# Two-layer cross-attention on one core: a new written-out order for the four engines, and one wait fewer

## The reference

```python
# layer 0 (x1 = x[b], x2 = ctx[b]); D = 64
q = x1^T Wq^T + bq ;  k = Wk x2 + bk ;  v = Wv x2 + bv
x = v @ softmax(q k)^T + x1
# layer 1 (CI = 256, no softmax, so it is linear)
g = g_w x2 + g_b ; theta = theta_w x + theta_b ; phi = phi_w x2 + phi_b
y = ((theta^T phi) / N) g^T ;  out = batchnorm(w_w y^T + w_b) + x
```

## Time and profile before

| | |
|---|---|
| median of 3 runs | 1082.88 us (1082.83 to 1083.77) |
| the profiled execution | 1082.83 us, span 1081.0 us |
| TensorE matmul busy | 1051.3 us, 97% of the span |
| VectorE, ScalarE, GpSimd busy | 688.5, 466.0 and 279.1 us |
| granted TensorE clock, mean | 0.997 of full speed |

### The profile page before, as it was taken

How to read it: one execution, slowest core, us unless ns; L and a number is a source line. 1 busy time by engine, 2 the same in 40 slices (tenths; PEclk the granted TensorE clock), 3 DMA queues, 4 the chain that set the end, 5 groups by cost and what they waited for, 6 DMA issues and landing times.

```text
span 1081.0 us, 14139 instructions
## 1 busy us (share of the span) xinstructions
PE 1051.3 (97%) x5272; PEld 871.0 (81%) x5272; DVE 688.5 (64%) x929; ACT 466.0 (43%) x794; POOL 279.1 (26%) x198
## 2 busy tenths in 40 slices
PE   5899999999999999999999999999999999999997
PEld 4688877888788887888878888788887888778886
DVE  6785387843878438773487735876368762787615
ACT  7543254433554345443544335443255432555411
POOL 0311243112521125112360114502254022440120
PEclk9999999999999999999999999999999999999999
DMA  8224352352513525136142442424424343243402
GB/s 284 98 72 132 118 175 67 73 152 99 191 44 76 163 93 176 46 82 204 60 156 59 110 163 69 147 71 110 151 78 137 78 115 139 84 136 74 137 20 78
DMA packets 80627, 122.07 MB, mean 113 GB/s; under 512 B 13104, under 2 KB 46384, under 8 KB 80560
## 3 DMA queue, kind: packets, MB, share of 16 engines
q1 hardware_dynamic: 80560, 121.17, 36.2%
HBM read 70.79 MB, written 16.78 MB: 81 GB/s over the span
## 4 chain that ended last, share of the span: by engine, by line
PE 83%; DVE 8%; DMA 5%; issue 2%; ACT 1%; SPq 0%; POOL 0%; DVEq 0%; ACTq 0%; POOLq 0%
PE pG L549 32%; PE pG L469 12%; PE pG L460 11%; PE pG L560 8%; DMA out_dram<-xr 4%; PE pG L489 4%; PE pS L501 3%; DVE xr L862 2%; PE pM L528 2%; PE pT L501 2%; PE pM L537 2%; DVE xr L857 2%; PE pT L450 1%; PE pT L570 1%; PE pG L570 1%
## 5 line engine op out<-in xcount | busy, mean ns | idle before, releaser
L549 PE MATMUL pG<-pt,vT 128*128 128x512 f32 x1536 | 352.6, 390 | 0.5 <-DVE pt L812 0.5
L549 PEld LDWEIGHTS pG<-pt,vT 128*128 128x128 f32 x1536 | 287.4, 188 | 59.7 <-issue 0.9
L460 PE MATMUL pG<-wv,x2s 128*128 128x512 f32 x768 | 183.1, 394 | 3.2 <-DVE vT L765 2.7
L460 PEld LDWEIGHTS pG<-wv,x2s 128*128 128x128 f32 x768 | 143.5, 189 | 36.7 <-DVE vT L765 5.7
L841 DVE SCALAR_TENSOR_TENSOR xr<-pG,cl,xr 128x512 f32<-128x512 f32 x64 | 48.0, 750 | 190.0 <-PE pG L549 185.9
L891 POOL TENSOR_TENSOR xms<-xr,xms 128x512 fp32r<-128x512 f32 x64 | 86.1, 1346 | 315.9 <-ACT xms L698 315.9
L469 PE MATMUL pG<-x2Ts 128*128 128x256 f32 (+2 forms) x768 | 129.3, 326 | 0.0
L469 PEld LDWEIGHTS pG<-x2Ts 128*128 128x128 f32 x768 | 115.7, 189 | 10.3 <-issue 2.9
L698 ACT ACTIVATE xms<-xr 128x512 fp32r<-128x512 f32 x64 | 40.3, 630 | 185.9 <-DVE xr L841 185.8
L883 POOL TENSOR_TENSOR x2Ts<-x2T_f,x2Ts 128x512 fp32r<-128x512 f32 x64 | 91.2, 1456 | 90.6 <-ACT x2Ts L645 90.5
L887 POOL TENSOR_TENSOR ys<-yf,ys 128x256 fp32r<-128x256 f32 x32 | 26.6, 830 | 310.2 <-ACT ys L666 309.7
(11 more groups left out here) (104 smaller groups left out, 1276.8 us busy)
## 6 DMA issues: line engine op xcount, KB each, us to landing
mv<-tp SPq DMA_DIRECT2D x512, 64.0 KB, 2.0
st<-in_ctx_dram SPq DMA_DIRECT2D x32, 512.0 KB, 5.8
st<-in_x_dram SPq DMA_DIRECT2D x32, 512.0 KB, 3.5
x2T_f<-in_ctx2T_dram SPq DMA_DIRECT2D x32, 512.0 KB, 6.0
xr<-in_x_dram SPq DMA_DIRECT2D x64, 256.0 KB, 3.2
out_dram<-xr SPq DMA_DIRECT2D x64, 256.0 KB, 2.7
wv_f<-in_wvT_dram SPq DMA_DIRECT2D x4, 256.0 KB, 6.5
wpg_f<-in_wpgT_dram SPq DMA_DIRECT2D x1, 1024.0 KB, 6.0
```

Of the source, the lines that this page charges most:

```text
L460: last = mm(bank, x2s[:, l, c, 128 * m:128 * m + 128], wv[:, r, c, :], start=(c == 0 and n == 0), stop=(c == 3 and n == 2))
L549: last = mm(bank, vT[:, l, m, 128 * c:128 * c + 128], pt(h)[:, r, m, :], start=(m == 0 and n == 0), stop=(m == 7 and n == 2))
```

## The change

All four order strings of `FIRST` and of `LATER` are replaced, and ScalarE's `do_q` loses a wait. No step is added or removed; only positions change, and for `x1:1` to `x1:3`, `x2:3` and `xs:3` the batch in whose string they stand. The parts near the end of a batch (`LATER`):

```diff
 pe (start of the batch)
-"q:0 k:0 q:1 k:1 v:0 gs v:1 v:2 S:0 S:1 gt G:0 S:2 S:3 G:1 G:2 GT:0 G:3 v:3 v:4 GT:1 S:4 S:5 v:5 ..."
+"k:0 q:0 q:1 k:1 v:0 v:1 v:2 gs S:0 S:1 G:0 S:2 S:3 G:1 G:2 gt G:3 v:3 S:4 S:5 GT:0 GT:1 v:4 v:5 ..."
 act (start)
-"x1:1 x1:2 x2:3 x1:3 xs:3 s q x2T:0 k x2T:1 x2T:2 x2T:3 v:0 x2T:4 x2T:5 x2T:6 q2 v:1 k2 gs x2T:7 v:2 gt ..."
+"q s x2T:0 x2T:1 k v:0 k2 q2 x2T:2 x2T:3 x2T:4 x2T:5 v:1 v:2 x2T:6 x2T:7 gs S:0 S:1 G:0 S:2 G:1 gt ..."
 act (end)
-"... PV:0,0 PV:0,1 T:4 T:5 T:6 T:7 B:0 B:1 PV:0,2 PV:0,3 PV:1,0 PV:1,1 PV:1,2 +x2:0 PV:1,3 +x2:1
- th:0,0 +xs:0 +x2:2 th:0,1 +xs:1 +x1:0 th:1,0 +xs:2 th:1,1"
+"... T:4 T:5 T:6 T:7 PV:0,0 PV:0,1 PV:0,2 PV:0,3 PV:1,0 PV:1,1 B:0 B:1 +x2:0 +x2:1 th:0,0 PV:1,2 +x2:2
+ PV:1,3 th:0,1 +xs:0 +xs:1 +x2:3 +xs:2 th:1,0 th:1,1 +x1:0 +x1:1 +x1:2 +x1:3 +xs:3"
 dve (start)
-"q k v:0 q2 k2 v:1 S:0 S:1 n:0 tr:0 v:2 n:1 tr:1 G:0 S:2 S:3 ..."
+"s q k v:0 k2 q2 v:1 v:2 S:0 S:1 n:0 tr:0 S:2 G:0 n:1 tr:1 G:1 S:3 ..."
 dve (end)
-"... B:0 B:1 PV:0,3 PV:1,0 PV:1,1 PV:1,2 PV:1,3 +x2:0 +x2:1 th:0,0 +x2:2 th:0,1 th:1,0 th:1,1
- wy:0,0 out:0,0 wy:0,1 out:0,1 wy:0,2 wy:0,3 wy:1,0 +x2:3 wy:1,1 out:0,2 out:0,3 out:1,0 out:1,1
- +s wy:1,2 wy:1,3 out:1,2 out:1,3"
+"... PV:0,3 PV:1,0 PV:1,1 PV:1,2 PV:1,3 B:0 B:1 +x2:0 th:0,0 +x2:1 +x2:2 th:0,1 th:1,0 th:1,1 +x2:3
+ wy:0,0 out:0,0 wy:0,1 out:0,1 wy:0,2 wy:0,3 out:0,2 out:0,3 wy:1,0 wy:1,1 out:1,0 out:1,1
+ wy:1,2 wy:1,3 out:1,2 out:1,3"
 pool
-"x1:0 x1:1 x1:2 x1:3 x2T:0 ... PV:1,3"
+"x2T:0 ... PV:1,3 +x1:0 +x1:1 +x1:2 +x1:3"
```

`FIRST` changes in the same manner. At its start:

```diff
 pe
-"k:0 k:1 v:0 v:1 q:0 q:1 gs v:2 v:3 S:0 v:4 S:1 S:2 gt G:0 G:1 GT:0 S:3 S:4 G:2 ..."
+"k:0 k:1 v:0 v:1 q:0 q:1 v:2 v:3 gs S:0 S:1 gt v:4 S:2 G:0 S:3 G:1 G:2 G:3 GT:0 ..."
 dve
-"x2:0 x2:1 x2:2 w:0 x2:3 consts w:1 w:2 x1:0 w:3 w:4 x1:1 x1:2 w:5 x1:3 s v:0 k w:6 w:7 w:8 q v:1 k2 q2 v:2 ..."
+"x2:0 x2:1 x2:2 w:0 x2:3 consts w:1 x1:0 w:2 w:3 w:4 w:5 x1:1 x1:2 s k x1:3 v:0 v:1 w:6 w:7 w:8 q k2 q2 v:2 ..."
```

and at its end, on ScalarE and VectorE:

```diff
 act
-"... PV:1,2 +x2:0 PV:1,3 +x2:1 th:0,0 +xs:0 +x2:2 th:0,1 +xs:1 +x1:0 th:1,0 +xs:2 th:1,1"
+"... PV:1,0 +x2:0 +x2:1 PV:1,1 PV:1,2 th:0,0 B:1 PV:1,3 th:0,1 +xs:0 +x2:2 +x2:3 th:1,0 +xs:1 th:1,1
+ +x1:0 +x1:1 +xs:2 +xs:3 +x1:2 +x1:3"
 dve
-"... th:1,1 wy:0,0 out:0,0 wy:0,1 out:0,1 wy:0,2 wy:0,3 wy:1,0 +x2:3 wy:1,1 out:0,2 out:0,3 ..."
+"... +x2:0 +x2:1 th:0,0 B:1 th:0,1 +x2:2 +x2:3 th:1,0 th:1,1 wy:0,0 wy:0,1 out:0,0 wy:0,2 out:0,1
+ out:0,2 wy:0,3 out:0,3 wy:1,0 wy:1,1 ..."
```

The wait:

```diff
             def do_q(b):
                 wait(eng, "q", b, 1)
-                if b:
-                    wait(eng, "oa", b - 1, 3)
                 done(act(q1[0:64, :], pT[64:128, :, :], ACT.Copy), "t1q")
```

More of the change, by code:

```diff
@@ L80 @@
         "x2T:0 x2T:1 x2T:2 x2T:3 x2T:4 x2T:5 x2T:6 x2T:7 Y:0 Y:1 Y:2 Y:3 PV:0,0 PV:0,1 PV:0,2 PV:0,3 PV:1,0 "
-        "PV:1,1 PV:1,2 PV:1,3"
+        "PV:1,1 PV:1,2 PV:1,3 +x1:0 +x1:1 +x1:2 +x1:3"
     ),
@@ L86 @@
     pe=(
[4 rows of a table removed]
[4 rows of a table added]
     ),
     act=(
[4 rows of a table removed]
[4 rows of a table added]
     ),
     dve=(
[5 rows of a table removed]
[5 rows of a table added]
     ),
     pool=(
-        "x1:0 x1:1 x1:2 x1:3 x2T:0 x2T:1 x2T:2 x2T:3 x2T:4 x2T:5 x2T:6 x2T:7 Y:0 Y:1 Y:2 Y:3 PV:0,0 PV:0,1 PV:0,2 "
-        "PV:0,3 PV:1,0 PV:1,1 PV:1,2 PV:1,3"
+        "x2T:0 x2T:1 x2T:2 x2T:3 x2T:4 x2T:5 x2T:6 x2T:7 Y:0 Y:1 Y:2 Y:3 PV:0,0 PV:0,1 PV:0,2 PV:0,3 PV:1,0 "
+        "PV:1,1 PV:1,2 PV:1,3 +x1:0 +x1:1 +x1:2 +x1:3"
     ),
```

## The result

The changed kernel takes 1101.45 us (median of 4 runs, 1100.64 to 1102.7), the kernel before 1082.86 us on the same chip: a ratio of 1.0171, with a 95% interval from 1.0153 to 1.0188. It is slower by 18.6 us. The forecast was 1098 us, in a range of 1079 to 1106, with 0.76 for slower.

What follows compares the result with a forecast made beforehand. TensorE's matmuls, busy 97% of the span, were taken as the bound. Terms +18.0 (six boundaries), -0.6 (out of batch 0), -1.0 (start) and -1.4 (end) gave +15.0 on 1082.8: 1098 us, range 1079 to 1106.

Steps and rivals of the forecast that it cites:

- forecast case: VectorE and GpSimd block each other at batch boundaries, TensorE stalls; 1098 us, own range 1092 to 1103, chance 0.48.
- step 1: End of a batch: GpSimd's late PV tiles delay th:0,1's low part, so th:1,1 stalls 1.9 to 2.0 us.
- faster: Rival: VectorE and GpSimd don't meet at the boundary, only the cures are left; 1072 us, chance 0.18.
- middle: Rival: no stall before th:1,1, only the wy stalls, +1.4 us for each of six boundaries; 1088 us, chance 0.22.
- Six boundaries: Boundaries out of LATER: +3.0 us taken for each, +18.0 in all.
- the start: First batch: the 2.69 us stall goes, S:0 waits some 3 us instead; -1.0, between -2 and +2.
- the end: Last batch: two fewer out between the last matmul and the last two evictions; -1.4, between -1.5 and 0.
- the boundary out of batch 0: th:1,1 isn't held up, wy stalls are smaller, the 1.6 before S:0 goes; net -0.6, between -1.5 and +2.
- the worked-out +3.4: One boundary's sum: k:1 over 4.0 us later, less the 0.6 wait before S:0 that goes.
- a bound for `T:3`: DMAs some 3 us later make T:3 ready 0.2 us before to 0.4 after PV:0,0 wants it.
- Step 4: qhi, qlo, khi, klo ready about 6.6 us after k:1, before v and gs end, so the 0.6 before S:0 goes.
- The removed wait: The wait taken from do_q on ScalarE is always met by the new order: 0 us.

Runs made afterwards that it cites:

- pv_split_early: The changed kernel, but ScalarE splits PV:1,2 and PV:1,3 before and between x2:0 and x2:1 again in batches 1 to 7: 1092.61 us.
- x1_zero: The changed kernel, but GpSimd writes zeros into x1's low part by memset in batches 1 to 7 and reads nothing: 1079.2 us.
- starts_new: The changed kernel with ScalarE's and VectorE's batch ends (from PV:1,0 on) as in the kernel before, wait in do_q kept: 1110.2 us.
- out_behind_wy: The changed kernel, but out:0,2 and out:0,3 behind wy:1,0 and wy:1,1 on VectorE in batches 1 to 7, wait in do_q back: 1108.6 us.
- before_cured: The kernel before with, in batches 1 to 7, k:0 before q:0, and k2 before q2, both ahead of x2T tiles on ScalarE: 1081.49 us.
- cured_sp: before_cured with the next batch's loads x2T:2 and x2T:3 issued behind the stores of out:1,0 to out:1,3 in SP's queue: 1072.8 us.
- end_new: The kernel before with only the ends of the batches changed (ScalarE and VectorE from PV:1,0 on): 1120.33 us.

## Why the prediction was right

**The forecast case happened, at the places named.** TensorE waits before `th:1,1`, `wy:1,2` and `q:0`; four `out` of over 2 us stand at a boundary and not two; no wait of L501 on `klo`. The block between VectorE and GpSimd is shown by the run without GpSimd's reads, step 1 by `pv_split_early`. The "faster" and the "middle" case each needed one of these to be absent.

**The terms.** Six boundaries were set at +18.0 and came to +21.8; the start at -1.0 and came to -1.24; the end at -1.4 and came to -1.53; the boundary out of batch 0 at -0.6, and it came to +0.88. The total was set at +15.0 and came to +19.9 in the profiled executions. The mean period out of `LATER` is 135.4, where 134.8 was written.

Split at `S:0`, the terms tell something else (change against the kernel before, us; from `PV:0,0` to the first `th` nothing changes):

| | forecast | came to |
|---|---|---|
| first `th` to `S:0`, six boundaries | +18.0 (+20.4 as worked out) | +15.5 |
| first `th` to `S:0`, out of batch 0 | -0.6 | -0.83 |
| `S:0` to `PV:0,0`, batches 2 to 7 | 0 | +6.3 |
| `S:0` to `PV:0,0`, batch 1 | 0 | +1.68 |

So the boundaries cost less than was worked out, the middles of the batches cost 8.0 us that the sum didn't have, and the two errors partly cancel. That the total came within 4 us of 1101.45 is in part luck: with the middles in it, the same sum would have been 1106, the upper end of the range. The boundary out of batch 0 itself came out as forecast, although `wy:1,3` waits 1.53 us there (at 150.35) for `wy:0,3`, which stands behind three `out`, two of them blocked; what makes it +0.88 is the middle of batch 1.

**Within a boundary** the worked-out +3.4 up to `S:0` was too much: it is 2.57 in the one followed. Step 1 was put at 1.9 to 2.0 and is 1.28 against the kernel before. Most of that error can be read: GpSimd starts 0.17 us sooner than worked out, and the blocked instructions follow each other every 1.1 us (three from 538.87 to 542.18) and not every 1.23 to 1.29. From start to start, `wy:1,2` waits 1.0 (forecast 1.3) and `q:0` 1.6 (forecast 1.7; the list of waits has 1.45).

**The term that was mis-sized is the middle of the batch**, set at 0 with 0.4 as a bound for `T:3`. TensorE never waits for `T:3`. It has two parts. The first is the new order itself, 0.54 us a batch: in `x1_zero` the middle takes 43.12 us in every batch, against 42.58. A piece of it is seen directly: before, `S:6` and `S:7` go together; after, each stands alone. TensorE before, then after:

```profile
602.54 0.50 PE L501 MATMUL pS<-khi,qhi 64*128 64x512 f32 x2
```

```profile
611.23 0.50 PE L501 MATMUL pS<-khi,qhi 64*128 64x512 f32 x2
612.13 1.70 PE L489 MATMUL pG<-wpg,gram 128*128 128x256 f32 x12
613.76 0.50 PE L501 MATMUL pT<-khi,qhi 64*128 64x512 f32 x2
614.65 4.58 PE L489 MATMUL pG<-wpg,gram 128*128 128x256 f32 x36
```

That is 0.90 + 1.63 + 0.89 = 3.42, against 3.10 before (1.52 of `Y:0`, and 1.58 from 602.54 to the next step at 604.12). The rest is spread over `v` and `G`, which take 0.1 to 0.2 more each in this batch.

The second part is a chain: `x2T:2` to `x2T:5` now stand behind `khi` on ScalarE, `khi` waits for the stores of `out:1,2` and `out:1,3`, and the end of `G:0` comes late. The longer `khi` waits in a batch, the longer the middle takes (the changed kernel, us):

| batch | 1 | 2 | 3 | 4 | 5 | 6 | 7 |
|---|---|---|---|---|---|---|---|
| `khi` waits for a store | 2.35 | 2.15 | 2.05 | 1.31 | 2.10 | 1.42 | 1.71 |
| middle, more than before | 1.68 | 1.40 | 1.26 | 0.57 | 1.39 | 0.72 | 0.98 |

In `starts_new`, which has the same middle, `khi` waits for a store in one batch alone, 4.15 us. That batch takes 44.4 us and the others 43.1 to 43.2. Step 4 had `khi` ready by the engines' work alone and left out that it waits for a store. `S:0` didn't pay for that in the changed kernel, since the late `q:0` covered it, but the middle did; in `out_behind_wy` and `before_cured` `S:0` pays as well. The batch followed in the timelines, batch 4, is the one where it shows least.

**The start.** The 2.69 us stall is gone, and the one expected in its place came, 2.6 us before `S:0`, with the low clock behind it: `S:0` starts at 36.48 and `G:0` at 43.62, where 36.5 and 43.7 were worked out. Windows of the changed kernel (length, busy, granted clock):

```profile
36.50:39.70 3.20, 3.20 (x15) 0.51 0.71 268
```

At 0.51, the 1.2 GHz level, after TensorE had stood still since about 33.9. The slow stretch of the earlier trace rows has only moved; the start gained by the shorter stalls, not by the clock. But 1.24 is the difference of two traces, and the same order doesn't repeat to better than that. With the new first batch `PV:0,0` starts at 77.0 to 77.6 us in four traces, where the clock stays up, and at 78.7 to 79.2 in six, where it falls; with the old one at 78.9 in one, where it stays up, and at 79.0 to 80.2 in three, where it falls. So the new start gains on average, by no more than whether the clock falls is worth.

**The removed wait.** In the changed kernel `out:0,3` is over at 559.7 and `q` is copied at 565.11, as soon as its matmuls are done; the wait would have been met 5 us earlier. It was not run by itself.

## What to carry to other kernels

Where VectorE and GpSimd work at the same time, place their instructions by what they read: a VectorE instruction with two inputs in SBUF costs what is left of GpSimd's instruction, and everything behind it on VectorE, evictions that TensorE waits for above all, pays too. A new order changes which wait is last, so each gain asks what is late next; here a store behind four loads ate two sound moves until SP's queue was changed as well. And one string of such an order can't be judged, or put back, without the others.

## What the runs showed of the hardware

- An `out` (128x512, both inputs in SBUF) takes 0.75 us alone, 0.75 beside a GpSimd memset, and 2.1 to 2.5 beside a GpSimd subtraction of 128x1024. Two engines that both have such work waiting take turns, one instruction each: `PV:1,2`, `x2:1`, `PV:1,3`, `x2:2` of GpSimd and VectorE fill 537.57 to 542.18.
- A store of 256 KB behind four loads of 512 KB was through about 8.5 us after its data was ready (566.3 to about 575); with two loads ahead it was through 2.8 us sooner in `cured_sp`'s batch than in `before_cured`'s, counted from `v:0` (555.51 - 550.51 = 5.0 and 562.89 - 555.12 = 7.8).
- A group of six matmuls with 64 rows takes 0.8 us beside another such group (twelve in 1.59) and 0.9 between groups of 128 rows.
- Stalls of 3.0 us before `q:0` in `end_new` were followed by a granted clock of 0.50 for 3.4 to 6.8 us in five boundaries of seven; those of 1.45 in the changed kernel never were.
